# Value products in one double batch per eight units, and the projection halves moved around it

## The reference, cut to what matters

```
k = key_value @ Wk + bk            # (4, 4096, 256), heads of 16
v = key_value @ Wv + bv
attn = softmax(clip(q k^T * scale))   # (4, 16, 256, 4096)
x = attn v, then @ Wo + bo
```

## Time and profile before

| | |
|---|---|
| median of three executions | 1292.84 us |
| profiled execution, its own time | 1290.42 us |
| its span, first to last instruction | 1288.6 us |
| TensorE busy | 1199.8 us, 93% |
| VectorE busy | 857.0 us, 67% |
| ScalarE busy | 729.3 us, 57% |
| mean granted TensorE clock | 0.965 of full |

### The profile page before, as it was taken

The page is one execution under the profiler, slowest core; times in us unless marked ns, Lnnn a source line. Parts: engine busy times, 40 slices in busy tenths (PEclk is TensorE's granted clock), DMA queues, the critical chain, the costliest instruction groups (busy, mean ns, idle before and its releaser), DMA issues.

```text
span 1288.6 us, 26107 instructions
## 1 busy us (share of the span) xinstructions
PE 1199.8 (93%) x10230; PEld 720.6 (56%) x10230; DVE 857.0 (67%) x1564; ACT 729.3 (57%) x1327; POOL 162.5 (13%) x198
## 2 busy tenths in 40 slices
PE   5899999999999999999999999997999889789776
PEld 4585555656565656565555555553555456455534
DVE  4667777777777777777777777786888036853443
ACT  2132666767676767676666667675777842234211
POOL 5432121111111111111111110010000041000100
PEclk9898999999999999999999999998999999899866
DMA  9672334343444434433344443226221000000000
GB/s 248 164 175 78 92 105 117 107 116 98 107 111 116 110 103 110 113 106 99 106 110 119 106 106 98 64 69 178 74 70 38 2 1 1 1 2 3 1 1 33
DMA packets 153330, 111.33 MB, mean 86 GB/s; under 512 B 18566, under 2 KB 152407, under 8 KB 153177
## 3 DMA queue, kind: packets, MB, share of 16 engines
q1 hardware_dynamic: 151577, 108.09, 31.8%
q10 hardware_dynamic: 1600, 1.31, 0.3%
HBM read 81.41 MB, written 27.79 MB: 85 GB/s over the span
## 4 chain that ended last, share of the span: by engine, by line
PE 85%; DVE 6%; ACT 4%; issue 2%; SPq 2%; DMA 1%; POOL 0%; DVEq 0%; ACTq 0%; POOLq 0%
PE acc L1360 20%; PE st L1319 19%; PE mx L1307 16%; PE kps L1267 7%; PE kps L1276 6%; PE st L1276 2%; ACT prob L813 2%; DVE kst L1090 1%; PE setB L1576 1%; PE kps L1307 1%; PE setB L1570 1%; PE st L1233 1%; PE acc L1267 1%; SPq L351 1%; PE st L1504 1%
## 5 line engine op out<-in xcount | busy, mean ns | idle before, releaser
L913 DVE TENSOR_REDUCE mxp<-mx 128x1 f32<-128x512 f32 x959 | 628.0, 686 | 239.0 <-PE mx L1307 235.6
L1319 PE MATMUL st<-qst,kst 99*128 99x256 bf16 x2048 | 390.0, 274 | 3.6 <-ACT prob L744 1.8
L1307 PE MATMUL mx<-kst,qst 96*128 96x512 bf16 x959 | 367.4, 383 | 20.3 <-DMA qst<-qscr 10.0
L744 ACT ACTIVATE prob<-st 128x512 f32<-128x512 f32 x512 | 288.7, 599 | 131.6 <-PE st L1319 130.8
L1319 PEld LDWEIGHTS st<-qst,kst 99*128 99x128 bf16 x2048 | 177.2, 98 | 213.9 <-issue 46.6
L744 ACT ACTIVATE xn<-st 128x512 f32<-128x512 f32 x256 | 144.6, 598 | 88.8 <-PE st L1319 88.8
L744 ACT ACTIVATE xnT<-st 128x512 f32<-128x512 f32 x256 | 150.4, 599 | 59.2 <-PE st L1319 56.5
L1360 PE MATMUL acc<-prob,v_raw 128*17 128x256 f32 x2048 | 135.4, 382 | 1.4 <-ACT prob L744 0.9
L1307 PEld LDWEIGHTS mx<-kst,qst 96*128 96x128 bf16 x959 | 92.6, 97 | 41.2 <-DMA qst<-qscr 10.4
L524 POOL CAST kraw<-kraw 128x512 bf16<-128x512 f32 x54 | 32.9, 610 | 627.7 <-DVE kraw L863 627.7
L1276 PE MATMUL kps<-wv,ctx 128*128 128x256 f32 (+1 forms) x376 | 96.8, 379 | 0.0
(11 more groups left out here) (360 smaller groups left out, 1048.8 us busy)
## 6 DMA issues: line engine op xcount, KB each, us to landing
kst<-kscr SPq DMA_DIRECT2D x128, 192.0 KB, 3.0
kst<-kscr SPq DMA_DIRECT2D x384, 64.0 KB, 2.8
kscr<-kraw SPq DMA_DIRECT2D x108, 192.0 KB, 2.7
ctx<-in_ctxT SPq DMA_DIRECT2D x93, 128.0 KB, 2.6
ctx<-in_ctxT SPq DMA_DIRECT2D x93, 64.0 KB, 2.4
kscr<-o_sb SPq DMA_DIRECT2D x20, 192.0 KB, 2.6
v_raw<-in_ctxT SPq DMA_DIRECT2D x3, 512.0 KB, 6.8
qscr<-v_raw SPq DMA_DIRECT2D x12, 128.0 KB, 2.1
```

Of the source, the lines that this page charges most:

```text
L744: act.activation(exps(n), st[n % 3][:, :], ACT.Exp).then_inc(exp_done, 1)
L913: dve.reduce_max(at, bank_of_max(n)[:, :], AX.X).then_inc(max_red, 1)
L1307: pe.matmul(bank_of_max(n)[:, :], qst[0:96, 4 * (q % 3) + j, qt * P:(qt + 1) * P], kst[0:96, j, at:at + 512], start=True, stop=True).then_ ...
L1319: mm = pe.matmul(st[n % 3][:, h * T:(h + 1) * T], kst[0:99, j, at:at + P], qst[0:99, 4 * (q % 3) + j, :], start=True, stop=True)
```

## The change

The value products of eight units are issued together, at t % 8 == 3 of the next block of eight: two calls of `values`, 16 matmuls, 32 records. The first half of a projection moves from t % 8 == 0 to 5, the second from 4 to 0 of the next block. ScalarE's copy out of `kps` moves from t % 8 == 5 to 1 of the next block, VectorE's `k_rest` from 6 to 2. The third bank for maxima starts four units later. The last two value batches stand behind the loop.

```
-NP = 11 * UQ + 48 + AHEAD
+NP = 11 * UQ + 52 + AHEAD
...
+        def block_before(n):
+
+            return (n // 8 - 1) // 8, (n // 8 - 1) % 8
...
-                if t % 8 == 5:
-                    c = k_job(q, t // 8)
+                if t % 8 == 1 and n >= 8:
+                    c = k_job(*block_before(n))
                     if c is not None:
                         k_first(c)
-                    c = v_job(q, t // 8)
+                    c = v_job(*block_before(n))
                     if c is not None:
                         v_copy(kps, c)
...
-                if t % 8 == 6:
-                    c = k_job(q, t // 8)
+                if t % 8 == 2 and n >= 8:
+                    c = k_job(*block_before(n))
                     if c is not None:
                         k_rest(c)
...
-                if n >= 4 and t % 4 == 2:
-                    values((n - 4) // UQ, (n - 4) % UQ // 4)
+                if n >= 8 and t % 8 == 3:
+                    for half in range(2):
+                        values((n - 8) // UQ, (n - 8) % UQ // 8 * 2 + half)
                 if t == 8 and q > 0:
                     finish(q - 1)
-                if t % 8 in (0, 4):
-                    g = t % 8 // 4
+                if t % 8 == 5:
                     c = k_job(q, k)
                     if c is not None:
-                        if g == 0:
-                            pe.wait_ge(*k_ctx_sem(c))
-                            pe.wait_ge(k_r, c)
-                            pe.wait_ge(v_out, VLEAD + 4 * q + k // 2)
-                        project_k(kps, ctx4[:, c % 2, :, :], g)
+                        pe.wait_ge(*k_ctx_sem(c))
+                        pe.wait_ge(k_r, c)
+                        pe.wait_ge(v_out, VLEAD + 4 * q + k // 2)
+                        project_k(kps, ctx4[:, c % 2, :, :], 0)
...
+                if t % 8 == 0 and n > 0:
+                    c = k_job(*block_before(n))
+                    if c is not None:
+                        project_k(kps, ctx4[:, c % 2, :, :], 1)
+                    c = v_job(*block_before(n))
+                    if c is not None:
+                        project_v(kps, ctx4[:, 2 + c % 2, :, :], 1)
...
+            values(NQ - 1, 14)
             values(NQ - 1, 15)
```

More of the change, by code:

```diff
@@ L1426, in _ @@
                     spread_low(q, 1)
-                if n >= 4 and t % 4 == 2:
-                    values((n - 4) // UQ, (n - 4) % UQ // 4)
+                if n >= 8 and t % 8 == 3:
+                    for half in range(2):
+                        values((n - 8) // UQ, (n - 8) % UQ // 8 * 2 + half)
                 if t == 8 and q > 0:
                     finish(q - 1)
-                if t % 8 in (0, 4):
-                    g = t % 8 // 4
+                if t % 8 == 5:
                     c = k_job(q, k)
                     if c is not None:
-                        if g == 0:
-                            pe.wait_ge(*k_ctx_sem(c))
-                            pe.wait_ge(k_r, c)
-                            pe.wait_ge(v_out, VLEAD + 4 * q + k // 2)
-                        project_k(kps, ctx4[:, c % 2, :, :], g)
+                        pe.wait_ge(*k_ctx_sem(c))
+                        pe.wait_ge(k_r, c)
+                        pe.wait_ge(v_out, VLEAD + 4 * q + k // 2)
+                        project_k(kps, ctx4[:, c % 2, :, :], 0)
                     c = v_job(q, k)
                     if c is not None:
[L1442 to L1446, removed]
+                        pe.wait_ge(*v_ctx_sem(c))
+                        pe.wait_ge(k_r, min(KLEAD + 4 * q + k // 2 + 1, NCH))
+                        pe.wait_ge(v_out, c)
+                        project_v(kps, ctx4[:, 2 + c % 2, :, :], 0)
+                if t % 8 == 0 and n > 0:
[5 more added lines that the diff above has]
+                        project_v(kps, ctx4[:, 2 + c % 2, :, :], 1)
                 if t == 59 and q + 1 < NQ:
```

## The result

| | before | changed |
|---|---|---|
| median | 1292.69 us (4 runs) | 1333.33 us (4 runs) |
| ratio to before | | 1.0319 (95%: 1.0305 to 1.0333) |
| profiled span | 1288.6 us | 1330.9 us |

The account below looks back on a forecast made before the run. TensorE's queue was taken to bound the kernel. Passes 0 to 10 +29, pass 11 +1, units 758 to 947 +7, last 76 units +4, late key block -0.5: 40.5, taken as 40, giving 1332.5 us, range 1317 to 1342.

Parts of the forecast that it names:

- TensorE's own queue sets the time, and every microsecond that it spends or waits more is paid in full: Whole kernel: TensorE busy 93% of the span; VectorE waits for it, its matmuls never for VectorE from 200 to 795 us.
- the price list: TensorE's timeline costs: unit 0.44 us, projection half 0.87, value batch 1.08, of which 0.21 is entering and leaving column groups.
- What the merge saves: Each double value batch takes 1.95 us instead of 2.16: 0.21 per block of eight units, 27 us if nothing else moved.
- What the runs of three cost: At t = 3 and t = 0 of every block the maximum matmul waits 0.29 us for its bank, 0.58 in all.
- the agreement on the waits that the prediction claims with the Trainium skill: The skill's PSUM Bottleneck: tiling speeds up matmuls but not the emptying of PSUM, which can then be the limit.
- The later stretches: From unit 758 to 947, eight-unit runs take 5.96 us, +7 us; the last 76 units take 5.21 per eight, +4 us.
- The wait for the late key block: Pass 12: a wait of 7.24 us, of which the slower pace takes up to 1 us; counted as -0.5.
- the term of 4: Last 76 units, scores only: 5.21 us per eight units against 4.80, as TensorE's longer absence starves ScalarE; +4 us.
- Pass starts: At each pass's first block `spread_low` stands between units 1 and 2 and takes 0.22 us off the wait: 2.4 us.
- the changeovers decide and the waits don't come: Rival, at each double batch, t = 3: -27 us, 1266, faster; chance 5%.
- only one of the two runs of three pays: Rival, projection stretch: one wait, say at t = 0, is taken back; 25.5 us less, 1307; chance 6%.
- the merge saves nothing: Rival: the 0.21 us hangs on key tiles or semaphores, is paid twice anyway, and waits stay; +27, 1359; chance 5%.

Follow-up runs that it names:

- s2_merge_only: The kernel before with only the double value batch at t = 3; projections, copies and third bank left where they were: 1368.1 us, ratio 1.060.
- t3_mix: Changed kernel with the second projection half cut in two and double value batches only to the end of pass 10, single ones after: 1274.7 us, ratio 0.987.
- t2_cut_batches: The kernel before with each value batch cut into its two key tiles, issued after t % 4 == 2 and 3: 1336.6 us, ratio 1.035.
- s1_split: Changed kernel with the second projection half cut into two matmuls, after unit 7 and after unit 1 of the next block: 1285.5 us, ratio 0.994.
- s4_half_after: Changed kernel with VectorE's maximum over the first 256 of 512 columns, for measurement only: 1274.8 us, ratio 0.987.
- s3_move_only: Changed kernel with value batches back to one per four units, so only the projections' move remains: 1313.4 us, ratio 1.016.
- u2_double_to_pass10: Changed kernel with double value batches only to the end of pass 10, then one per four units; projections as changed: 1322.4 us, ratio 1.024.

## Why the prediction was right

**The number.** That 1332.5 lies within 1 us of 1333.3 is in part luck. The differences by stretches add up to 43.2 us for a forecast 40.5, and each of the four is off by 0.4 to 1.2 us. What carries is the mechanism, stretch by stretch.

**What bounds.** The step "TensorE's own queue sets the time, and every microsecond that it spends or waits more is paid in full" held: in every run the blocks between a pass's ends came out as the price list says, within 0.04 us, but for the key blocks of s2_merge_only.

**What the merge saves.** 0.21 us per changeover was right: 1.95 us for the double batch in the changed kernel, 7.22 us for a block without waits in t3_mix, and 0.22 more per added changeover in t2_cut_batches.

**What the runs of three cost.** 0.29 twice was right to the hundredth (0.73 where 0.44 is free, 7.79 to 7.80 us for a forecast 7.80). It is shown by three opposite edits: breaking the runs (s1_split), shortening what they wait for (s4_half_after), and taking one of the two away (s3_move_only). The banks waited for are those of the full-width maximum matmuls; in the list of waits of the changed kernel no column-tiled batch waits for an emptied bank, so the agreement on the waits that the prediction claims with the Trainium skill is not one that this case shows.

**The later stretches.** 5.96 and 5.21 us per eight units came as worked out. That passes 12 to 14 came out at 6.1 us for a forecast 6.5 is in part luck. The wait for the late key block, 7.24 us before, is 5.04 us:

```profile
922.79 0.61 PE L1311 MATMUL kps<-kst,qst 96*128 96x512 bf16 x1 [5.04 <-DMA kst<-kscr]
```

That is 2.2 us less, where the prediction had 0.5. The rest of these passes lost 8.3 us, where it had 7. In u2_double_to_pass10 this wait is 6.7 us, with the same passes 0 to 10 but single batches behind them, which points to the slower pace of passes 11 and 12; that was not tested by itself.

Pass 15 with the last batch is 1.2 us above the term of 4, and here it is the clock (a window of 2 us, columns as in the earlier trace rows, granted clock 0.50):

```profile
1048.00:1050.00 2.00, 2.00 (x15) 0.99 (x17) 0.56 (x3) 1.42 (x3) 0.00 (x0) 0.50 0.00 0
```

The granted clock falls to half (1.2 GHz) early in the pass; from 1040.8 to 1046 us, still at full, TensorE had been busy 4.51 of 5.2 us. In s1_split, with the same double batches in this pass, the clock stays at full and the stretch takes 44.2 us, 3.6 more than before, which bears the term out. The two batch distances in which the clock is low are 7.16 and 5.79 us, against 6.12 and 5.21 there, and that is the whole difference of 1.6.

**Pass starts** were sized a little too kind (2.74 us forecast per pass, 2.9 measured). The 0.22 taken off for `spread_low` does appear: the block over a pass's boundary grows by 0.15 us (8.09 before, 8.24 after) and not by 0.37. But the next one grows by 0.57 (8.09 to 8.66), and in it stands `finish`, which the prediction did not look at; why it costs more there stays open. s3_move_only shows the same weak point with the other sign: what stands between units only at a pass's ends was counted by eye.

**A slip in the sum.** 1330.4 + 2.4 is 1332.8, and not 1332.5; it changes nothing.

**What the prediction did not need, and had only half right:** it said that the residual of the key chunk is hidden after the move. It is, but the prediction did not say that this is a gain of the move over the merge alone, 0.49 us per key chunk. s2_merge_only missed by 18 us for that.

Of the rivals, "the changeovers decide and the waits don't come", "only one of the two runs of three pays" and "the merge saves nothing" all fell on the block time of 7.80 with 149 waits and a double batch of 1.95 us.

## What to carry to other kernels

When an engine fills a ring of n banks and another empties it, write down two numbers: the time between fills in a row, and the time from a fill to the release of its bank. If n fills in a row are shorter than the release, every run longer than n waits, even if the emptying engine is idle a third of the time. Three banks cover that release here (three fills are 1.32 us, the release 1.17), and yet a run of eight waits, since VectorE needs 0.60 us per bank and TensorE 0.44: the number of banks sets how long a run goes free, and beyond that every fill costs the difference of the two paces. So other work belongs between the fills in pieces, with two banks one piece for every pair of fills; merging pieces to save a changeover lengthens the runs, and here each 0.21 us saved cost 0.58. Cutting another piece in two gave the saving without the waits.

## What the runs showed of the hardware that was not expected

Going into and out of the column groups costs the same 0.21 us for 8, 16 and 32 records. An fp32 projection half cut into its two matmuls, with a bf16 unit between them, costs nothing that the block time shows: 7.22 us is 8 x 0.44 + 1.95 + 1.74 to 0.01.

The short fall of the granted clock in pass 15 of the changed kernel cost 1.6 us and is missing in s1_split and in the kernel before. A difference of 2 us in one stretch of one execution is worth a look at the clock before it is given another cause.
